# An audio tower on one core: every engine's calls written out row by row in another sequence

## The reference, cut to what matters

```python
h = gelu(x @ W1 + b1); h = gelu(h @ W2 + b2)
lens = sigmoid(h @ W3 + b3); lens = lens / sum(lens) * 375
P = maximum(cumsum(lens)[:, None] - arange(375), 0)    # -> weights of a warp
h = warp(P) @ x                                        # 750 tokens -> 375
xn = rmsnorm(layernorm(h)); q, k, v = xn @ w_qkv       # 8 heads of 64, 8 memory keys
h = h + rmsnorm(softmax(q) @ (softmax(k) @ v) @ w_out + b_out)
xf = layernorm(h); route = argmax(xf @ switch.T + b)   # 16 experts
h = h + where(pos < capacity, xf @ expert[route] + eb[route], xf) * prob
```

## Time and profile before

| | |
|---|---|
| median of 3 runs | 394.02 us (393.65 to 394.21) |
| span of the profiled execution, first to last instruction | 392.4 us |
| its time as a run | not listed apart; the runs lie 1.3 to 1.8 us above the span |
| PE busy | 374.4 us, 95% of the span |
| DVE busy | 335.1 us, 85% |
| ACT busy | 227.2 us, 58% |
| POOL busy | 111.8 us, 28% |
| mean granted TensorE clock | 0.996 of full speed |

### The profile page before, as it was taken

The page is one execution under the profiler, slowest core; times in us unless marked ns, Lnnn a source line. Parts: engine busy times, 40 slices in busy tenths (PEclk is TensorE's granted clock), DMA queues, the critical chain, the costliest instruction groups (busy, mean ns, idle before and its releaser), DMA issues. The chain is left out here.

```text
span 392.4 us, 7891 instructions
## 1 busy us (share of the span) xinstructions
PE 374.4 (95%) x2702; PEld 327.1 (83%) x2702; DVE 335.1 (85%) x916; ACT 227.2 (58%) x433; POOL 111.8 (28%) x136
## 2 busy tenths in 40 slices
PE   8999899999999999999999999999999989999892
PEld 8887788888889888888988888888887788998892
DVE  4687869969897999799988999899998975888896
ACT  4653369627971699159933994389537743782200
POOL 6121301031152216221522141403330501107880
PEclk9999999999999999999999999999999999999998
DMA  7768002002000110002000200100000070331134
GB/s 222 193 197 272 2 1 85 3 0 82 5 20 3 27 62 22 3 0 85 14 10 1 86 7 15 47 0 3 22 0 0 22 195 7 89 118 33 41 80 126
DMA packets 16406, 21.58 MB, mean 55 GB/s; under 512 B 4930, under 2 KB 11928, under 8 KB 15934
## 3 DMA queue, kind: packets, MB, share of 16 engines
q1 hardware_dynamic: 12398, 18.30, 16.1%
q0 software_dynamic: 2880, 2.35, 2.4%
q10 hardware_dynamic: 1088, 0.42, 0.4%
HBM read 14.40 MB, written 6.62 MB: 54 GB/s over the span
## 5 line engine op out<-in xcount | busy, mean ns | idle before, releaser
L1093 PE MATMUL psB<-W2h,h1l 128*125 128x512 f32 x184 | 74.6, 406 | 0.0
L1094 PE MATMUL psB<-W2l,h1h 128*125 128x512 f32 x184 | 72.5, 394 | 0.0
L1095 PE MATMUL psB<-W2h,h1h 128*125 128x512 f32 x184 | 72.5, 394 | 0.0
L668 ACT ACTIVATE h2b<-h2b 125x512 f32<-125x512 f32 x48 | 30.0, 628 | 30.9 <-DVE h2b L1640 30.5
L1095 PEld LDWEIGHTS psB<-W2h,h1h 128*125 128x125 f32 x184 | 34.1, 185 | 8.5
L1094 PEld LDWEIGHTS psB<-W2l,h1h 128*125 128x125 f32 x184 | 34.2, 186 | 6.9
L1093 PEld LDWEIGHTS psB<-W2h,h1l 128*125 128x125 f32 x184 | 34.2, 186 | 6.9
L1640 DVE TENSOR_TENSOR h2b<-psB,b2r 125x512 f32<-125x512 f32 x48 | 32.8, 685 | 4.5 <-PE psB L1095 4.4
L651 ACT ACTIVATE h<-psA,b1c 128x376 f32<-128x376 f32 x60 | 33.3, 579 | 5.7 <-PE psA L1040 3.9
L1647 DVE CUSTOM_DVE_ANT_0 h2b<-h2b,W3r 125x512 f32<-125x512 f32 x48 | 32.9, 690 | 1.6 <-ACT h2b L668 1.4
L531 POOL TENSOR_TENSOR dx<-xt 125x640 f32<-125x640 f32 x8 | 12.9, 1617 | 64.6 <-PE psC L1118 53.0
(11 more groups left out here) (284 smaller groups left out, 970.0 us busy)
## 6 DMA issues: line engine op xcount, KB each, us to landing
xTf<-in_x_t SPq DMA_DIRECT2D x16, 187.5 KB, 2.5
xt<-in_x SPq DMA_DIRECT2D x8, 336.0 KB
slot_x<-eb_parts SPq DMA_DIRECT2D x2, 960.0 KB, 11.9
basef<-in_L_tok_W SPq DMA_DIRECT2D x4, 256.0 KB, 5.3
ewT<-in_expert_t SPq DMA_DIRECT2D x1, 1024.0 KB, 8.0
ewf<-slot_x SPq DMA_DIRECT2D x2, 480.0 KB, 6.2
h2b<-slot_x SPq DMA_DIRECT2D x2, 480.0 KB, 8.2
slot_y<-h SPq DMA_DIRECT2D x4, 240.0 KB, 2.4
```

The costliest lines, as they stand in the source:

```text
L668: nc.scalar.activation(slot, slot, ACT.Gelu).then_inc(c_g2.sem, 1)
L1093: mm(ps, lo, W2h[:, k, :], start=k == 0, stop=False)
L1094: mm(ps, hi, W2l[:, k, :], start=False, stop=False)
L1095: last = mm(ps, hi, W2h[:, k, :], start=False, stop=k == HK - 1)
```

## The change

`pipeline`, `step`, `opening` and `ending` go away on GpSimd, ScalarE, TensorE and VectorE. Each of the four engines gets one flat list of the same calls with row numbers written in. SP's list stays. No helper changes, but for two that take in a wait which was a call of its own (`memory_keys` on ScalarE and `sums` on TensorE call `setup()` for row 0). The instructions are the same ones; only their order on each engine differs.

GpSimd: the old step, and the new list (rows 2 to 5 repeat the pattern of row 1):

```diff
 
-def pipeline(opening, step, ending):
-
-    opening()
-    step(2, 1, 0, None)
-    for b in range(2, LAST - 1):
-        step(b + 1, b, b - 1, b - 2)
...
 
-    def step(m, f, k, r):
-        if f is not None:
-            sigmoid_pow(f, before(f))
-        if r is not None:
-            scatter(r, before(r))
-        if m is not None:
-            differences(m, before(m))
-        if f is not None:
-            norm1(f, before(f))
-        if k is not None:
-            norm2(k, before(k))
-            norm3(k, before(k))
-            counts(k, before(k))
 
```

```diff
+    differences(0, None)
+    sigmoid_pow(0, None)
+    differences(1, 0)
+    norm1(0, None)
+    sigmoid_pow(1, 0)
+    norm1(1, 0)
+    norm2(0, None)
+    norm3(0, None)
+    counts(0, None)
+    differences(2, 1)
+    scatter(0, None)
+    sigmoid_pow(2, 1)
+    norm1(2, 1)
+    norm2(1, 0)
+    norm3(1, 0)
+    counts(1, 0)
...
+    sigmoid_pow(6, 5)
+    norm1(6, 5)
+    norm2(5, 4)
+    norm3(5, 4)
+    counts(5, 4)
+    scatter(5, 4)
+    differences(7, 6)
+    norm1(7, 6)
+    norm2(6, 5)
+    norm3(6, 5)
+    counts(6, 5)
+    fetch(2, 0, 3)
+    fetch(1, 0, 1)
+    fetch(1, 1, 3)
+    fetch(0, 0, 3)
+    fetch(3, 0, 3)
+    fetch(4, 0, 3)
+    fetch(5, 0, 3)
```

ScalarE: the opening's end, a row step, the ending:

```diff
+            setup()
         copy(bank_k(b, p)[:, 1 + G:1 + NK], mk[:, p, :]).then_inc(c_mk.sem, 1)
 
...
+    gelu1(1, 0, 1, 3)
+    h1_upper(1, 0, 1)
+    gelu2(1, 0)
+    gelu2(1, 1)
+    take_h(0, None)
+    xn_hi(0, None)
+    gelu2(1, 2)
+    gelu2(1, 3)
...
+    route_exp(0, None)
+    gelu2(2, 4)
+    gelu2(2, 5)
+    gelu1(3, 2, 0, 0)
+    gelu1(3, 2, 0, 1)
+    take_kt(1, 0, 0)
+    gelu1(3, 2, 0, 2)
+    gelu1(3, 2, 0, 3)
+    take_kt(1, 0, 1)
+    take_kt(1, 0, 2)
+    h1_upper(3, 2, 0)
+    gelu1(3, 2, 1, 0)
+    gelu1(3, 2, 1, 1)
+    take_ctx(1, 0)
+    gelu1(3, 2, 1, 2)
+    gelu1(3, 2, 1, 3)
+    take_qt(1, 0, 0)
+    take_qt(1, 0, 1)
+    take_qt(1, 0, 2)
+    h1_upper(3, 2, 1)
+    x_hi_next(3)
+    take_h(2, 1)
+    gelu2(3, 0)
+    xn_hi(2, 1)
+    take_v(2, 1, 0)
+    take_v(2, 1, 1)
+    take_v(2, 1, 2)
...
+    memory_keys(6, 3)
+    gelu2(7, 4)
+    gelu2(7, 5)
+    key_exp(6, 5, 3)
+    own_sigmoid(7, 6)
+    take_kt(6, 5, 0)
+    take_kt(6, 5, 1)
+    take_kt(6, 5, 2)
+    take_qt(6, 5, 0)
+    take_ctx(6, 5)
+    take_qt(6, 5, 1)
+    take_qt(6, 5, 2)
+    take_h(7, 6)
+    take_tokens(0)
+    take_tokens(1)
+    memory_keys(7, 0)
+    xn_hi(7, 6)
+    take_outputs(0)
```

TensorE: the opening, a row step, the ending twice:

```diff
+        if prev is None:
+            setup()
         after(pe, c_s, b, 2)
...
+    layer1(1, 0, 1, 2)
+    layer1(1, 0, 1, 3)
+    layer2(1, 0, 1)
+    warp(0, None)
+    layer2(1, 0, 2)
+    layer2(1, 0, 3)
+    xn_transposed(0, None)
+    values(0, None, 0)
+    values(0, None, 1)
+    values(0, None, 2)
+    queries(0, None, 0)
+    keys(0, None, 0)
+    queries(0, None, 1)
...
+    positions(0, 1)
+    layer2(2, 1, 5)
+    k_transposed(1, 0, 0)
+    layer1(3, 2, 0, 0)
+    layer1(3, 2, 0, 1)
+    k_transposed(1, 0, 1)
+    k_transposed(1, 0, 2)
+    layer1(3, 2, 0, 2)
+    layer1(3, 2, 0, 3)
+    layer1(3, 2, 1, 0)
+    layer1(3, 2, 1, 1)
+    sums(2, 1)
+    context(1, 0)
+    q_transposed(1, 0, 0)
+    q_transposed(1, 0, 1)
+    q_transposed(1, 0, 2)
+    layer1(3, 2, 1, 2)
+    layer1(3, 2, 1, 3)
+    layer2(3, 2, 0)
+    fold(1, 0, 2)
+    warp(2, 1)
+    attend(1, 0)
+    layer2(3, 2, 1)
...
+    keys(6, 5, 2)
+    layer2(7, 6, 4)
+    layer2(7, 6, 5)
+    keys(6, 5, 3)
+    keep_clock()
+    k_transposed(6, 5, 0)
+    k_transposed(6, 5, 1)
+    k_transposed(6, 5, 2)
+    sums(7, 6)
+    q_transposed(6, 5, 0)
+    context(6, 5)
+    q_transposed(6, 5, 1)
+    q_transposed(6, 5, 2)
+    fold(6, 5, 7)
+    warp(7, 6)
+    attend(6, 5)
+    expert_tokens(0)
+    xn_transposed(7, 6)
+    expert_tokens(1)
+    expert_products(0)
+    expert_products(1)
...
+    expert_tokens(6)
+    k_transposed(7, 6, 0)
+    k_transposed(7, 6, 1)
+    positions(6, None)
+    expert_tokens(7)
+    k_transposed(7, 6, 2)
+    expert_products(5)
+    expert_products(6)
+    expert_products(7)
+    context(7, 6)
+    q_transposed(7, 6, 0)
+    q_transposed(7, 6, 1)
+    chosen_on_rows(6)
+    q_transposed(7, 6, 2)
+    fold(7, 6, None)
+    dense_bias(6)
+    attend(7, 6)
+    dense(6, 0)
+    dense(6, 1)
```

VectorE: the opening, a row step, and the ending:

```diff
+    lengths(0, None)
+    warp_weights(0, None)
+    split_weights()
+    h1_lower(1, 0, 1)
+    bias2(1, 0, 1)
+    moments1(0, None)
+    bias2(1, 0, 2)
+    normal1(0, None)
+    dot3(1, 0, 0)
+    keep_h(0, None)
+    bias2(1, 0, 3)
+    xn_lo(0, None)
+    x_lo_next(1)
+    dot3(1, 0, 1)
+    dot3(1, 0, 2)
...
+    key_max(1, 0, 2)
+    key_max(1, 0, 3)
+    place_in_expert(0, None)
+    key_sum(1, 0)
+    dot3(2, 1, 2)
+    dot3(2, 1, 3)
+    bias2(2, 1, 4)
+    bias2(2, 1, 5)
+    dot3(2, 1, 4)
+    dot3(2, 1, 5)
+    minus_z(2, 1)
+    query_sum(1, 0)
+    scan(2, 1)
+    query_norm(1, 0)
+    lengths(2, 1)
+    h1_lower(3, 2, 0)
+    keep_h(1, 0)
+    warp_weights(2, 1)
+    take_m(1, 0)
+    probability(0, None)
+    keep_base(0, None)
+    x_lo_next(3)
+    h1_lower(3, 2, 1)
+    moments1(2, 1)
+    bias2(3, 2, 0)
+    normal1(2, 1)
+    out_norm(1, 0)
...
+    bias2(7, 6, 4)
+    bias2(7, 6, 5)
+    key_max(6, 5, 3)
+    dot3(7, 6, 4)
+    dot3(7, 6, 5)
+    query_norm(6, 5)
+    scan(7, 6)
+    key_sum(6, 5)
+    lengths(7, 6)
+    warp_weights(7, 6)
+    take_m(6, 5)
+    probability(5, 4)
+    keep_base(5, 4)
+    moments1(7, 6)
+    normal1(7, 6)
+    out_norm(6, 5)
+    xn_lo(7, 6)
+    residual(6, 5)
+    moments2(6, 5)
+    query_max(7, 6, 0)
+    query_max(7, 6, 1)
+    query_max(7, 6, 2)
+    normal2(6, 5)
+    key_max(7, 6, 0)
+    key_max(7, 6, 1)
...
+    probability(6, 5)
+    query_norm(7, 6)
+    place_in_expert(6, 5)
+    take_outputs(5)
+    keep_h(7, 6)
+    keep_base(6, 5)
+    spread_choice(6)
+    key_sum(7, 6)
+    take_outputs(7)
+    own_experts(6)
+    own_tokens(6, 0)
+    take_m(7, 6)
+    own_tokens(6, 1)
+    own_tokens(6, 2)
+    own_tokens(6, 3)
+    own_tokens(6, 4)
+    own_tokens(6, 5)
+    own_tokens(6, 6)
+    own_tokens(6, 7)
+    out_norm(7, 6)
+    own_norm2(7, 6)
+    residual(7, 6)
+    moments2(7, 6)
+    own_tokens(6, 8)
...
+    take_logits(7, 6)
+    own_tokens(6, 15)
+    route(7, 6)
+    spread_choice(7)
+    own_counts(7, 6)
+    own_experts(7)
+    own_tokens(7, 0)
+    probability(7, 6)
+    own_tokens(7, 1)
...
+    own_tokens(7, 12)
+    own_tokens(7, 13)
+    finish_row(6)
+    place_in_expert(7, 6)
+    finish_row(0)
+    keep_base(7, 6)
+    own_tokens(7, 14)
+    own_tokens(7, 15)
+    finish_row(1)
+    finish_row(2)
+    finish_row(7)
+    finish_row(3)
+    finish_row(4)
+    finish_row(5)
```

More of the change, by code:

```diff
@@ new lines, in _ @@
+            layer1(4, 3, 1, 0)
+            layer1(4, 3, 1, 1)
+            sums(3, 2)
+            q_transposed(2, 1, 0)
+            q_transposed(2, 1, 1)
+            q_transposed(2, 1, 2)
+            layer1(4, 3, 1, 2)
+            layer1(4, 3, 1, 3)
+            layer2(4, 3, 0)
+            fold(2, 1, 3)
+            warp(3, 2)
+            attend(2, 1)
+            layer2(4, 3, 1)
+            xn_transposed(3, 2)
+            layer2(4, 3, 2)
+            values(3, 2, 0)
+            values(3, 2, 1)
@@ new lines, in _ @@
+            k_transposed(3, 2, 1)
+            k_transposed(3, 2, 2)
+            layer1(5, 4, 0, 2)
+            layer1(5, 4, 0, 3)
+            context(3, 2)
+            layer1(5, 4, 1, 0)
+            sums(4, 3)
+            layer1(5, 4, 1, 1)
+            layer1(5, 4, 1, 2)
+            q_transposed(3, 2, 0)
+            layer1(5, 4, 1, 3)
+            q_transposed(3, 2, 1)
+            q_transposed(3, 2, 2)
+            layer2(5, 4, 0)
+            fold(3, 2, 4)
+            warp(4, 3)
+            attend(3, 2)
@@ new lines, in _ @@
+            layer2(6, 5, 0)
+            fold(4, 3, 5)
+            layer1(6, 5, 1, 3)
+            warp(5, 4)
+            attend(4, 3)
+            layer2(6, 5, 1)
+            xn_transposed(5, 4)
+            layer2(6, 5, 2)
+            values(5, 4, 0)
+            values(5, 4, 1)
+            values(5, 4, 2)
+            queries(5, 4, 0)
+            queries(5, 4, 1)
+            queries(5, 4, 2)
+            xf_transposed(4, 6)
+            layer2(6, 5, 3)
+            logits(4, 6)
+            keys(5, 4, 0)
@@ new lines, in _ @@
+            q_transposed(5, 4, 1)
+            q_transposed(5, 4, 2)
+            layer1(7, 6, 1, 1)
+            fold(5, 4, 6)
+            layer1(7, 6, 1, 2)
+            layer1(7, 6, 1, 3)
+            warp(6, 5)
+            attend(5, 4)
+            layer2(7, 6, 0)
+            xn_transposed(6, 5)
+            layer2(7, 6, 1)
+            keys(6, 5, 0)
+            values(6, 5, 0)
+            values(6, 5, 1)
+            values(6, 5, 2)
+            xf_transposed(5, 7)
+            queries(6, 5, 0)
@@ new lines, in _ @@
+            scan(3, 2)
+            h1_lower(4, 3, 0)
+            lengths(3, 2)
+            probability(1, 0)
```

(32 more changed lines are left out.)

1553 lines of the change are left out of this document (794 added, 759 removed).

## The result

The kernel got slower: 396.59 us (median of 4 runs, 395.77 to 397.69) against 394.12 beside it, a ratio of 1.0067 with a 95% interval of 1.0047 to 1.0087. The profiled execution is the slowest of the four, 397.69, with a span of 396.0 us; the others have spans of 394.0 to 394.9.

The account below looks back on a forecast made before the run. PE bounds the middle, chains through VectorE and ScalarE the two ends. From a median of 394.02 us, -0.6 + 1.4 - 1.4 - 1.15 + 0.3 = -1.45, rounded to -1.5, gave 392.5 us; range 389.7 to 396.2.

Parts of the forecast that it names:

- The scatters ahead of `sigmoid_pow`: Row steps, GpSimd: three scatters delay sigmoid_pow, 5.2 + 1.3 = 6.5 us; VectorE's scan waits 0.8 at worst in one step.
- the bounds of the middle: Row steps: loss from ScalarE's order around the key copies, between 0 and 1.1 us a step.
- the clock gives and takes nothing: Whole kernel: granted clock 1.00 in every stage where PE works, so no time gained or lost by it.
- The gathers: Kernel end: gathers start 2.3 us later, last lands at 387.1, taking back 0.3 us and capping any larger gain.
- The end: From `own_experts` on: VectorE's waits of 0.88 and 0.63 us get covered; minus 1.15 us, bounds minus 1.5 and 0.
- plus 0.3: Kernel end: the 0.3 us that the later gathers take back from the gain.
- The opening: Up to row 0's first `values`: PE's 1.7 us xn wait goes, partly returning for xl; minus 0.6 us, bounds minus 1.7 to 0.
- The row steps: Middle: ScalarE's order around the key copies makes PE wait, 0.35 us in each of four steps; plus 1.4 us.
- rival 2: Row steps: ScalarE's new order holds PE, 1.1 us a step in five steps, loss 5.5 us; 396.7 us, chance 0.23.
- 269 to 331: Up to row 7's transposes: `memory_keys` wait goes and gaps around the warp fill; minus 1.4 us, between 0 and minus 2.4.
- the first three terms: Opening, row steps and 269 to 331: minus 0.6, plus 1.4 and minus 1.4 us.
- Rival 1: Stretched VectorE calls beside GpSimd hold PE, so removing the stretch gives 2.2 us more; 390.3 us, chance 0.12.

Follow-up runs that it names:

- the run with the power call first: The new kernel with sigmoid_pow put ahead of the scatter right before it in each of five steps; 395.15 us, 1.0035.
- the run with the one swap: The new kernel with row 2's sigmoid_pow put ahead of row 0's scatter, in the step at 107 us only; 395.60 us, 1.0035.
- the first try to bring the gathers forward: The new kernel with the last three expert products ahead of row 7's key transposes and their evictions earlier on ScalarE and VectorE; 397.27 us, 1.0088.

## Why the prediction was wrong

It said 392.5 us, and faster with 0.58; the time was 396.59, 0.4 above the range. Two steps failed: what it said of the calls that come late next on GpSimd, and where it put the gathers.

- **The scatters ahead of `sigmoid_pow`.** The step said "a wait of 0.8 at worst in one step, else none", and let PE's cover for it lie within the bounds of the middle. It put the queue at 6.5 us. In the step at 107 us it took 7.38: the three scatters and the power call as sized, but 0.90 us more from the end of the VectorE call that the scatter waits for (100.77 and 0.17) to the first scatter, which the sum left out. VectorE had calls for 6.38 us of it and waited for 1.00; it waited 0.72 and 0.25 in two other steps. (Its two waits of 1.26 us are not the scatters': they are there with the power call first, too, as 1.23 and 1.22.) PE had no cover in that one step and stood idle for 1.20. So the size was nearly right; what was wrong is that it was priced at nothing, and that "the clock gives and takes nothing", which was read from an order that had no such wait there. With the fall to 0.50 behind it in some executions, this step costs 1.4 us by the medians of the run with the power call first, 1.0 by those of the run with the one swap, and 1.3 by the ratios of both.
- **The gathers.** The step put their start 2.3 us later and took 0.3 us off the gain. They started 6.25 us later. 2.9 us of that is PE's order, as worked out. PE came 2.7 us late to `chosen_on_rows` (356.77 against 354.08), not 0.6 early, which is 3.3 more; and 0.7 us lies between the last product and the first gather: 0.3 of it as the eviction stands behind `keep_h`, `keep_base`, `spread_choice` and `key_sum`, 0.4 from the last store's issue to the gather (4.14 us, 3.77 before). The last gather then took 4.8 us to land, not 3.6. That PE's lateness is not the whole is shown by the run in which the power call comes first: PE is there on time (354.10), and VectorE waits 3.54 us all the same. The end as a whole, minus 1.15 plus 0.3 in the sum, cost 1.4 us in the new order (395.15 against 393.80) and 2.5 in the old (396.23 against 393.74); "plus 0.3" is the term that was mis-sized. If the filled waits gave their 1.15, it was 2.5 to 3.6 us, an estimate from these runs.

With both undone, the new order takes 393.80 us, which can't be told from the kernel before (0.9999). So the two account for the whole loss, and what is left of the change is worth nothing, where the terms beside the end came to minus 0.6.

The other steps stood better. **The opening:** the 1.7 us wait for xn went, and a wait for xl came in its place:

```profile
49.90 0.50 PE L1178 MATMUL psC<-Wql,xh 128*128 128x512 f32 x1 [1.16 <-DVE xl L1980]
```

With 0.6 us more ahead of `sums`, PE is idle as long as before; but it starts that call, with the same calls ahead of it, 1.4 us earlier than at 51.32. Of this, 0.65 us is a start of the program that differs between runs (one of the first products of `layer1` begins at 6.63 against 7.28). That leaves 0.8, where 0.6 was taken: this term was right. **The row steps:** ScalarE's order was not the trouble; the waits before `context` are three, 0.9 us in all, where there were five of 1.3. That is against rival 2, though its sign came true: the lost time came from GpSimd and VectorE. With the scatters mended PE is idle for 2.8 us in the middle, 1.6 more than before; 1.4 was predicted, for another reason, in part the power call beside `query_norm`. **269 to 331:** 1.55 us less idle time with the scatters mended (minus 1.4 predicted), and the wait for `memory_keys` is gone from the list. At the row 7 transposes that kernel stands 0.9 us ahead (330.28 against 331.22), of which 0.7 is the start of the program, so 0.2 is left; the first three terms gave 0.6. **The end:** VectorE's waits of 0.88 and 0.63 us are gone, as predicted, its wait for row 6's `chosen_on_rows` grew from 0.75 to 1.75, and the gathers took back more than was won.

**Rival 1** (the collisions are on the path) is refuted as a gain of this change: the six weight calls take 2.03 or 2.04 us in every step of the new kernel and the first `h1_lower` 1.72, so the stretch is gone, and the time is longer. (In four of the steps before, it was 0.18 us, not "0.2 to 0.3".) With the power call first in all five steps the weight calls are stretched again (2.29 to 2.68), with the one swap they are not in the other four, and both have the ratio 1.0035. What the shorter `h1_lower` gave in the opening was not taken apart. That the old order's collisions are hidden does not make collisions free: the runs show three on the path, `dot3` beside late differences (0.29 us a step), the weight calls beside differences a step late (2 us a step), and the power call beside `query_norm` (2.83 us against 1.33), which the new order made itself. The last agrees with what the Trainium skill says, in SBUF — State Buffer, section Who interferes with whom: a VectorE call with two SBUF inputs contends with a GpSimd call that reads SBUF.

## What to carry to other kernels

Where two engines' lists are fitted to one another, a list is not good or bad by itself: the same GpSimd list cost 0 us with one order of the other engines and 11 with another, and calls taken out of one collision can land in a dearer one. Before moving calls to avoid collisions, ask which later call on the same queue has somebody waiting for it; a short call that starts a chain (here a power call of 1.33 us) goes ahead of long DMA issues that nobody needs yet. When a queue is set against the work that covers it, count the time from the call that releases it to its first call as well; here it was 0.8 to 0.9 us. And follow a late producer to the end of its queue of transfers: 18 gathers that are issued one after another move the end of the kernel by as much as their first one is late, once their slack is used up.

## What was not expected of the hardware

- A wait of 1.20 us on PE, with the short matmuls of `context` behind it, was followed by a granted clock of 0.50 for some 3 us in the new kernel, and by 1.00 in the first try to bring the gathers forward, where the same calls stand around it. In the old order with GpSimd's new list, of four waits of 1.05 us only the last was followed by a fall (0.50 from 243 to 246 us), and a wait of 1.62 us ahead of `sums` at 285.5 was, too (0.57 from 288 to 291). The wait of 1.7 us in the opening before was not: the clock is 1.00 in that stage.
- The last gather lands 4.7 to 5.2 us behind its issue in the six kernels in which VectorE waited over 3 us for it (those with the new end, whatever GpSimd's order or the steps before it), and 3.9 in the kernel before. Stores of the output were issued while the last gathers were under way, in the new kernel (from 383.08 us) and in the kernel before (from 379.78); whether these slow them was not tried.
- A power call of 125x6 elements that starts 0.1 us behind a VectorE call of 125x1536 takes 2.83 us instead of 1.33: it ends 1.19 us behind that call, as if it had begun when the other ended.
